# Layer 0 of a two-layer block on one core: the same steps in another order on TensorE, ScalarE, VectorE and GpSimd

## The reference

```python
x_proj, z = split(layernorm(x) @ in_proj_W)
# window scan, 4 tokens, 8 states, 384 channels, forward and backward
dt = silu(dt_raw @ dt_W + dt_b)
state = exp(dt * a_n) * state + dt * b_n * x      # per token, per state n
y += state * c_n
y_conv = gelu(dwconv3x3(x_proj) @ pw_W)
y = (alpha * y_ssm + (1 - alpha) * y_conv) * silu(z) @ out_W
x_out = x + y
x_out += gelu(layernorm2(x_out) @ fuse_W1 + fuse_b1) @ fuse_W2 + fuse_b2
```

## Time and profile before

| | us |
|---|---|
| median of 3 runs | 4693.17 |
| the profiled execution: time | 4693.32 |
| its span | 4691.5 |
| layer 0, from the start to the first table load of layer 1 | 2622.9 |
| busy over the span: PE, DVE, POOL, ACT | 4396.0, 3877.0, 3675.9, 3348.8 |
| mean granted TensorE clock | 0.979 of full |

### The profile page before, as it was taken

The page is one execution under the profiler, slowest core; times in us unless marked ns, Lnnn a source line. Parts: engine busy times, 40 slices in busy tenths (PEclk is TensorE's granted clock), DMA queues, the critical chain, the costliest instruction groups (busy, mean ns, idle before and its releaser), DMA issues. The chain is left out here.

```text
span 4691.5 us, 79419 instructions
## 1 busy us (share of the span) xinstructions
PE 4396.0 (94%) x24320; PEld 3132.4 (67%) x24320; DVE 3877.0 (83%) x7295; ACT 3348.8 (71%) x5828; POOL 3675.9 (78%) x3476
## 2 busy tenths in 40 slices
PE   5899999999999999999998799999999999999998
PEld 3556565656565656565655578878878778878887
DVE  4999989999999999999998477777777777777775
ACT  5898988898989888989885255555555555555555
POOL 4898989898989898989897366667666676766666
PEclk7999999999999999999999799999999999999999
DMA  2011111111111111111101400040001300040000
GB/s 82 25 37 47 36 46 37 48 35 48 35 49 34 49 34 49 34 49 34 49 28 43 128 22 16 19 116 25 22 22 42 93 22 20 21 121 22 15 19 19
DMA packets 139268, 198.15 MB, mean 42 GB/s; under 512 B 18346, under 2 KB 106388, under 8 KB 138644
## 3 DMA queue, kind: packets, MB, share of 16 engines
q1 hardware_dynamic: 138900, 193.76, 13.0%
HBM read 114.02 MB, written 79.69 MB: 41 GB/s over the span
## 5 line engine op out<-in xcount | busy, mean ns | idle before, releaser
L1294 POOL TENSOR_TENSOR pl<-probs,ph 128x512 fp32r<-128x512 f32 x1024 | 1322.8, 1292 | 646.2 <-PE ps_o L1404 323.1
L748 POOL TENSOR_TENSOR dec<-dt,rates 128x384 f32<-128x384 f32 x1536 | 1514.8, 1017 | 244.3 <-ACT dt L634 188.7
L1497 ACT ACTIVATE ph<-ps_s 128x512 fp32r<-128x512 f32 x1024 | 613.6, 599 | 904.2 <-PE ps_s L1387 897.1
L1509 DVE TENSOR_REDUCE part_max<-ps_m 128x1 f32<-128x512 f32 x1024 | 687.7, 688 | 393.9 <-PE ps_m L1370 393.9
L1396 PE MATMUL ps_o<-ph,vh 128*128 128x512 f32 x2048 | 812.4, 397 | 18.0 <-ACT o_ch L1483 17.7
L1396 PE MATMUL ps_o<-ph,vl 128*128 128x512 f32 x2048 | 805.6, 393 | 0.0
L1538 DVE TENSOR_TENSOR ps_a<-probs,ps_a 128x512 f32<-128x512 f32 x992 | 681.3, 687 | 40.9 <-ACT probs L1499 35.4
L1404 PE MATMUL ps_o<-pl,vh 128*128 128x512 f32 x2048 | 635.0, 391 | 0.0
L1499 ACT ACTIVATE probs<-ps_s 128x512 f32<-128x512 f32 x1024 | 606.8, 593 | 0.0
L906 DVE SCALAR_TENSOR_TENSOR psS<-u,bc,psS 128x384 f32<-128x384 f32 x1024 | 597.7, 612 | 1.2
L915 DVE SCALAR_TENSOR_TENSOR y_tok<-psS,bc,y_tok 128x384 f32<-128x384 f32 x960 | 552.5, 605 | 4.5
(11 more groups left out here) (166 smaller groups left out, 7669.3 us busy)
## 6 DMA issues: line engine op xcount, KB each, us to landing
values_d<-hid SPq DMA_DIRECT2D x64, 512.0 KB, 4.3
xf<-in_x_dram SPq DMA_DIRECT2D x128, 128.0 KB
xb<-in_x_dram SPq DMA_DIRECT2D x128, 128.0 KB
residual_d<-xb SPq DMA_DIRECT2D x32, 512.0 KB, 2.7
vh<-values_d SPq DMA_DIRECT2D x32, 512.0 KB, 7.3
vl<-values_d SPq DMA_DIRECT2D x32, 512.0 KB, 9.4
res<-residual_d SPq DMA_DIRECT2D x32, 512.0 KB, 3.3
out_dram<-res SPq DMA_DIRECT2D x128, 128.0 KB
```

Source lines behind the costliest of these rows:

```text
L748: last = nc.gpsimd.tensor_tensor(dec[:, q % RING, j - 1, :], dt[:, par, d, token_of(d, j), :], rates[:, d, n, :], ALU.mult)
L1294: nc.gpsimd.tensor_tensor(pl[:, m % DEPTH, :], probs[:, m % DEPTH, :], ph[:, m % DEPTH, :].bitcast(F32), ALU.subtract).then_inc(pl_ok, 1)
L1497: nc.scalar.activation(ph[:, m % DEPTH, :], ps_s[m % 2][:, :], ACT.Exp).then_inc(ph_ok, 1)
L1509: nc.vector.tensor_reduce(part_max[:, qt, kc:kc + 1], ps_m[r % 2][:, :], AX.X, ALU.max).then_inc(max_out, 1)
```

## The change

The four tables are replaced; no instruction, wait or function is added or removed. Since the banks follow from `PE_ORDER`, the bank of some front steps changes too, and with it which step each of them waits for.

```diff
 PE_ORDER = """
-    z0 z1 yt0- yt1- yt2- z2 out0- conv0a out1- conv1a conv2a conv0b conv0c conv1c conv2c xnt0+ h2t0- h2t1- xnt1+
-    pw0 w10- xnth+ pw1 w11- proj+ pw2 inx0+ w12- inx1+ w13- inx2+ dtf0+ dtb0+ w20- inx3+ w21- dtf1+ dtb1+ inx4+
-    x1t0- dtf2+ dtb2+ x1t1- inx5+ dtf3+ dtb3+ fg0- xk0+ xk1+ xk2+ v0- bct+ v1-
+    z0 z1 yt0- yt1- yt2- z2 out0- out1- conv0a conv1a conv2a conv0b conv0c conv1c conv2c h2t0- h2t1- xnt0+ xnt1+
+    pw0 w10- w11- xnth+ pw1 w12- pw2 w13- proj+ inx0+ inx1+ w20- inx2+ dtf0+ dtb0+ w21- dtf1+ dtb1+ x1t0- inx3+
+    dtf2+ dtb2+ x1t1- inx4+ dtf3+ dtb3+ xk0+ inx5+ xk1+ fg0- xk2+ v0- bct+ v1-
 """.split()
 ACT_ORDER = """
-    exp1 ln1_std+ exp2 ow exp3 z0 z1 ln1_norm+ z2 exp4 ln2_std- exp5 ln2_norm- conv0c conv1c conv2c xnt0+ exp6
-    h2t0- h2t1- xnt1+ exp7 exp8 pw0 w10- xnth+ pw1 w11- exp9 proj+ exp10 pw2 inx0+ w12- inx1+ w13- exp11 inx2+
-    exp12 dtf0+ dtb0+ exp13 inx3+ exp14 dtf1+ dtb1+ inx4+ x1t0- dtf2+ dtb2+ x1t1- inx5+ dtf3+ dtb3+ exp15 fg0-
-    xk0+ xk1+ xk2+ exp0+ v0- bct+ v1-
+    exp1 ln1_std+ ow exp2 exp3 z0 z1 ln1_norm+ z2 exp4 ln2_std- exp5 ln2_norm- conv0c conv1c conv2c exp6 h2t0-
+    h2t1- xnt0+ exp7 xnt1+ exp8 pw0 w10- w11- exp9 xnth+ exp10 pw1 w12- pw2 w13- proj+ exp11 inx0+ inx1+ exp12
+    inx2+ dtf0+ dtb0+ exp13 exp14 dtf1+ dtb1+ x1t0- inx3+ dtf2+ dtb2+ x1t1- inx4+ dtf3+ dtb3+ exp15 xk0+ inx5+
+    xk1+ fg0- xk2+ v0- exp0+ bct+ v1-
 """.split()
 DVE_ORDER = """
-    st0 ln1_stats+ st1 ln1_mean+ st2 yt0- st3 yt1- st4 ln1_rstd+ st5 yt2- st6 ln1_shift+ st7 st8 st9 out0- st10
+    st0 ln1_stats+ ln1_mean+ st1 st2 st3 ln1_rstd+ yt0- st4 st5 ln1_shift+ yt1- yt2- st6 st7 st8 st9 out0- st10
     out1- ln2_stats- ln2_mean- st11 st12 ln2_rstd- st13 ln2_shift- st14 st15 st16 st17 st18 st19 st20 st21 st22
-    st23 st24 st25 st26 st27 st28 st29 st30 st31 st32 st33 st34 st35 st36 st37 st38 st39 w20- w21- st40 st41
-    st42 st43 st44 st45 fg0- st46 st47 gd_mul+ v0- gd_sum+ v1-
+    st23 st24 st25 st26 st27 st28 st29 st30 st31 st32 st33 st34 st35 st36 w20- st37 st38 w21- st39 st40 st41
+    st42 st43 st44 st45 st46 fg0- st47 gd_mul+ v0- gd_sum+ v1-
 """.split()
 POOL_ORDER = """
-    arg2 arg3 umb0 acc0 arg4 acc1 arg5 umb1 umb2 acc2 arg6 acc3 arg7 acc4 arg8 umb3 acc5 arg9 acc6 arg10 acc7
-    arg11 acc8 arg12 acc9 arg13 acc10 arg14 acc11 arg15 acc12 arg0+ acc13 umf0+ umf1+ umf2+ umf3+ acc14 acc15
-    arg1+
+    acc14- acc15- umb0 arg2 arg3 umb1 umb2 umb3 acc0 arg4 acc1 arg5 acc2 arg6 acc3 arg7 acc4 arg8 acc5 arg9 acc6
+    arg10 acc7 arg11 acc8 arg12 acc9 arg13 acc10 arg14 acc11 arg15 acc12 acc13 arg0+ arg1+ umf0+ umf1+ umf2+
+    umf3+
 """.split()
```

## The result

The changed kernel takes 4718.84 us (median of 5 runs, 4717.42 to 4723.22) against 4693.29 before (the median of 5 too; 4693.17 is that of the first three); the ratio is 1.0055, with a 95% interval of 1.0045 to 1.0066. It is 25 us slower. The profiled execution took 4717.58 us, its span is 4715.8. The forecast was 4673, with 4612 to 4712 as its range: wrong in sign, and outside the range.

A forecast was written before the change was run, and what follows sets the result against it. Bound: one loop of engines waiting for each other, POOL `arg0` to `arg10`, then ACT `exp10` to `dt3`. Mean turn 77.73 becomes 76.65 + 0.4 = 77.05; 0.68 over 30 turns is 20 us: 4693.3 - 20 = 4673, range 4612 to 4712.

The forecast's parts named there:

- The reading of the old loop: POOL from `arg0` to `arg10`, ACT from `exp10` to `dt3`, then `arg0` again: 77.27 us.
- `exp10` would come at about 50: On ACT, `exp10` starts about 50 us into the turn, before 51.98; alone worth 2 us in the old loop.
- The chain over PE and ln2: From `dt3` over `xk2`, `z0`, `out1`, ln2, `h2t0` and `inx2` back to `dt3`; sets the turn at 76.7 us.
- A turn without a fall: One turn, `arg0` to `arg0`, in which TensorE's clock does not drop; forecast 76.65 us.
- About the same share of turns with a fall, 8 in 30: TensorE's clock drops in 8 of 30 turns at 1.47 us each, 0.4 in the mean turn.
- The waits near dt: PE waits about 0.7 us for `w21` on DVE and 1.0 for dt1, instead of 1.64 in one piece.
- Rival C: Clock falls in every turn, between dt1 and `inx5` on PE; 1.47 us each, 4705 us; chance 0.18.
- its point of decision: Share of turns with a clock fall from which the change is slower: 73 of 100; before it was 31.
- The rule on short pauses: The Trainium skill: TensorE's clock falls only after longer pauses than 1.64 us; by it no falls, sum 4661 us.
- ACT's 6.37 at `exp1`: ACT's wait of 6.37 us for POOL at `exp1`, forecast to go since `arg1` comes 8 us sooner.
- POOL's idle before `arg0`: POOL's wait before `arg0`, forecast to be put down to DVE's `z3` rather than ACT's dt.
- DVE's wait at `p1(15)`: DVE's wait before `p1(15)`, forecast at some 2 us; 3.22 before the change, for `exp15`.

The follow-up runs named there:

- a_st11_early: The changed kernel with the matmuls of `inx3` issued twice on TensorE, and `st11` moved ahead of `ln2_stats` and `ln2_mean` on VectorE; 4653.57 us.
- a_st11_no_fill: The changed kernel with `st11` moved ahead of `ln2_stats` and `ln2_mean` on VectorE, no step issued twice; 4686.96 us.
- b_x1t0_late: The old kernel with `x1t0` moved from before dt2 to after it on TensorE and ScalarE; 4748.39 us.

## Why the prediction was wrong

**The reading of the old loop was right.** `arg0` to `exp10`, then ACT to `dt3`, then `arg0`: this is the loop of both kernels, and where `exp10` moved by 0.71 (a_st11_early), the turn moved by 0.67.

**"`exp10` would come at about 50" failed.** It came at 51.91. I had counted POOL's own work and the waits that the old trace shows, and not looked for the next one to end last: a POOL that runs 2 us ahead reaches `acc2` before `z3(2)`, which VectorE has only at 1350.94, that is at 31.25 (before: 30.36). I had put DVE 1.35 us later at `out1` myself (0.9 measured, there and at `z3(2)`), counted it for ln2, and not asked who on POOL waits behind it. This is the term that was missing. a_st11_early takes this wait away and wins 0.71 of the 1.9; the rest stays, since `acc3` then waits 1.24 for `z3(3)`.

**The chain over PE and ln2** was forecast well as far as single steps go: `xk2` at 4.5 (4.62), its wait 1.1 (0.99), `z0` at 9.0 (8.98), `h2t0` at 37.15 (36.78) with 0.8 of wait (0.96), and ACT's stretch to `dt3`. As the bound it was wrong by half a microsecond: ACT reached `inx2` later than PE, not sooner, since `exp10` was late. A turn without a fall, forecast 76.65, is 77.18: 0.53 x 30 = 16 us.

**"About the same share of turns with a fall, 8 in 30" failed, and it carries the sign.** The waits near dt were 0.29 and 2.08 instead of 0.7 and 1.0. Against the forecast's times dt1 is moved out 0.7 late (72.6, not 71.9), and PE had `inx3` done 0.4 soon (70.5, not 70.9), since `w21` hardly held it up. But the late `exp10` doesn't make the wait. In a_st11_no_fill `exp10` comes at 51.20 and dt1 is moved out at 2307.57 - 2235.67 = 71.90, as forecast, and the wait is 2.09 all the same:

```profile
2235.67 5.79 POOL L748 TENSOR_TENSOR dec<-dt,rates 128x384 f32<-128x384 f32 x6 [2.15 <-ACT dt L634]
...
2303.78 0.63 PE L409 MATMUL psB<-ident,xb 128*128 128x128 f32 x4 [0.16 <-DVE xb L847]
2307.57 0.88 PE L486 MATMUL psF<-dt_w,proj_sb 48*128 48x384 f32 x3 [2.09 <-ACT dt L634]
```

PE's steps ahead of the wait came 0.7 sooner as well, so `inx3` was done at 69.8. What the forecast had wrong is where PE stands against ACT in this stretch: by 1.1 us. The falls followed: 27 turns of 30 have one. Rival C named the place and the price (1.47; 1.44 measured), and its point of decision, 73 of 100 turns, is passed. It gave 4705 because it stood on the forecast's 76.65; with 77.18 it would have given 4721. I gave it 0.18. It should have had more, since its condition hung on two differences of long sums that could err by half a microsecond each, and the step from 1.64 to a little more is enough: b_x1t0_late shows 10 falls become 25 with 0.44 us more of wait.

Together: the turn without a fall was 16 us too low over 30 turns, and the falls cost 30 x (78.55 - 77.18) = 41 us where the forecast had 12. That is 45 of the 46 us between 4673 and 4719.

**The rule on short pauses.** In the old kernel a pause of 1.64 us is followed by half the clock in a third of the turns, in the new one 2.08 (with 0.29 ahead of it) in nearly all, and with 0.33 to 1.41 left in that place none is. The Trainium skill (TensorE: Matmul & The Clock Gate, "Why this matters for your kernels") warns there of pauses over about 3 us only; these runs show that a kernel whose TensorE is 94% busy loses 19 us in the old order and 42 in the new one to shorter ones.

**The rest.** `out1` lost its wait, ACT's 6.37 at `exp1` went, and POOL's idle before `arg0` was never put down to `z3(13)`, but split: `acc13` waits 1.78 for it and `arg0` 0.61 for dt after that. It was hidden, as forecast. DVE's wait at `p1(15)`, forecast at some 2 us, is 3.42.

**What stays open.** Why 3 turns in 30 of the new kernel keep the full clock after the same wait (2.07 to 2.10 in all 30), and 20 in 30 of the old. The two turns shown are alike to a few hundredths of a microsecond up to the fall, so it isn't the work in them. The record of the clock narrows it. dt2 starts 72.6 us after `arg0` in every turn but the first (72.1). The half-speed stretch begins at 73.8 in the first of nine turns in a row that have one, 0.1 to 0.2 sooner in each that follows, and at 72.6 in the ninth; the next turn has none, and the one after it has its own at 73.8 again. So it goes with the place in the turn at which the clock's steps happen to come. No run moved that place by itself.

## What to carry to other kernels

Before moving steps, list every pause of TensorE in a turn and price the new ones twice: for the time, and for the clock. A pause that costs nothing, since another engine is the bound there, can cost 1.5 to 2 us if the clock falls behind it. An idle engine can be given its last step to do again at no cost: that, not the new order, was worth 0.4%, and with `st11` moved 0.8% (4653.57 us against 4693). When an engine gets ahead, ask for each of its waits who ends it next; the old trace names only those that ended last in the old order.

## What the runs showed of the hardware that was not expected

Issuing a step of 1.1 us twice on the busiest engine made the kernel 18.7 us faster in the old order and 41.6 in the new one.

The falls keep a step of their own. In the new kernel the half-speed stretches come at even distances of 78.5 us, up to nine in a row. A turn that has one takes 78.6 to 78.7, so the next stretch comes at nearly the same place of the next turn, and once a turn is hit, the next mostly is too. The distance is 78.5 as well in a_st11_no_fill, where a turn with a fall takes only 77.9 to 78.0: there the stretch comes about half a microsecond later in each turn, and after two or three turns one is free (153.6 us between two falls). That the match of turn and distance is why the new order has so many falls is an inference from these distances; no run tests it by itself. In the old kernel a turn with a fall, 78.74, is followed by one without in 7 of 10 cases.
